# Low-rank FFN: stacked fp32r parts of the first product, and the inner layer's product with 64-row halves

## The reference, cut to what matters

```
def _L1_ffn_ref(x, U1, V1, b1, U2, V2, b2):
    D_MODEL, D_FF, RANK = (256, 1024, 64)
    B, S = (4, 1024)
    P = jnp.einsum('bsd,dr->bsr', x, U1)
    H = jax.nn.gelu(jnp.einsum('bsr,rf->bsf', P, V1) + b1)
    Q = jnp.einsum('bsf,fr->bsr', H, U2)
    return jnp.einsum('bsr,rd->bsd', Q, V2) + b2
...
x = x + _L1_ffn_ref(_layernorm(x, axis=-1), L1_ffn_U1, ..., L1_ffn_b2)   # block six (s5F), block eight (s7F)
```

## Time and profile before

| | before |
|---|---|
| median of 3 runs | 3765.04 us |
| span of the profiled execution | 3759.3 us |
| TensorE matmul busy | 3174.3 us (84%) |
| VectorE busy | 2380.3 us (63%) |
| ScalarE busy | 2097.1 us (56%) |
| GpSimd busy | 844.5 us (22%) |
| mean granted TensorE clock | 0.93 |

### The profile page before, as it was taken

One profiled execution on the slowest core, in us unless ns is written; L12 is line 12 of the kernel. 1 busy time (PEld: TensorE's weight loads), 2 busy tenths in 40 slices (PEclk: granted clock), 3 DMA queues, 4 the chain that ended last, 5 costly groups with the idle time before them and its releaser, 6 DMA issues. The chain is left out here.

```text
span 3759.3 us, 71272 instructions
## 1 busy us (share of the span) xinstructions
PE 3174.3 (84%) x21288; PEld 2152.6 (57%) x21288; DVE 2380.3 (63%) x5292; ACT 2097.1 (56%) x3482; POOL 844.5 (22%) x1652
## 2 busy tenths in 40 slices
PE   6699999999999639996883599959688888797879
PEld 3366666666666339996441499944355555533433
DVE  4488888888886664444567644435477677435853
ACT  3589989898987224442221344422266666354544
POOL 2211111111110114443001244524422222120112
PEclk9899999999999769998896799979899899898889
DMA  3300000000000314433003244331211111100001
GB/s 116 101 22 25 25 25 22 25 25 25 22 24 16 113 52 90 90 79 74 9 0 113 66 92 91 73 81 62 83 51 51 47 52 52 24 0 12 0 18 39
DMA packets 148659, 186.76 MB, mean 50 GB/s; under 512 B 20304, under 2 KB 114768, under 8 KB 148560
## 3 DMA queue, kind: packets, MB, share of 16 engines
q1 hardware_dynamic: 123984, 151.94, 12.6%
q0 software_dynamic: 24576, 33.57, 5.5%
HBM read 122.54 MB, written 62.91 MB: 49 GB/s over the span
## 5 line engine op out<-in xcount | busy, mean ns | idle before, releaser
L1717 DVE CUSTOM_DVE_ANT_0 s0Ah_SD<-s0Ah_ps_s,s0Ah_table 128x1024 f32<-128x1024 f32 x512 | 623.3, 1218 | 40.1 <-PE s0Ah_ps_s L1808 25.2
L1763 ACT ACTIVATE s0Ah_PM<-s0Ah_SD,s0Ah_nb 128x1024 f32<-128x1024 f32 x512 | 594.6, 1161 | 24.6 <-POOL s0Ah_nb L1706 24.6
L1818 PEld LDWEIGHTS s0Ah_ps_t<-top_ident,s0Ah_PM 128*128 128x128 f32 x4096 | 480.8, 141 | 103.0 <-ACT s0Ah_PM L1763 3.4
L1818 PE MATMUL s0Ah_ps_t<-top_ident,s0Ah_PM 128*128 128x128 f32 x4096 | 533.8, 273 | 0.4
L1769 ACT COPY s0Ah_PT<-s0Ah_ps_t 128x512 f32<-128x512 f32 x512 | 302.9, 592 | 104.3 <-PE s0Ah_ps_t L1818 99.8
L2021 ACT ACTIVATE s4Ch_PM<-s4Ch_SD,s4Ch_nb 128x260 f32<-128x260 f32 (+2 forms) x512 | 254.3, 497 | 145.7 <-POOL s4Ch_nb L1964 132.3
L1808 PE MATMUL s0Ah_ps_s<-s0Ah_ks,s0Ah_qs 96*128 96x512 bf16 x1024 | 308.5, 383 | 28.2 <-DMA s0Ah_ks<-s0A_parts 27.5
L1725 DVE COPY s0Ah_PT<-s0Ah_ps_t 128x512 f32<-128x512 f32 x384 | 264.9, 690 | 94.7 <-PE s0Ah_ps_t L1818 91.9
L1706 POOL TENSOR_TENSOR s0Ah_nb<-s0Ah_mx,s0Ah_minus 128x1 f32<-128x1 f32 x512 | 98.2, 192 | 930.5 <-DVE s0Ah_mx L1717 930.5
L1831 PE MATMUL s0Ah_ps_v<-s0Ah_PT,s0Ah_Vs 128*32 128x512 f32 x2048 | 273.9, 607 | 0.0
L1975 DVE CUSTOM_DVE_ANT_0 s4Ch_SD<-s4Ch_ps_s,s4Ch_table 128x260 f32<-128x260 f32 (+2 forms) x512 | 205.1, 408 | 79.8 <-PE s4Ch_ps_s L2066 65.2
(11 more groups left out here) (389 smaller groups left out, 7432.8 us busy)
## 6 DMA issues: line engine op xcount, KB each, us to landing
s1M_raw_w<-in_L_ffn_w SPq DMA_DIRECT2D x16, 1024.0 KB
s3M_raw_w<-in_L_ffn_w SPq DMA_DIRECT2D x16, 1024.0 KB
s0A_parts<-s0Ap_sp SPq DMA_DIRECT2D x48, 256.0 KB, 2.4
s4C_parts<-s4Cp_sp SPq DMA_DIRECT2D x48, 256.0 KB, 2.4
s0Ah_qs<-s0A_parts SPq DMA_DIRECT2D x64, 96.0 KB
s0Ah_ks<-s0A_parts SPq DMA_DIRECT2D x64, 96.0 KB
s4Ch_qs<-s4C_parts SPq DMA_DIRECT2D x64, 96.0 KB
s4Ch_ks<-s4C_parts SPq DMA_DIRECT2D x64, 96.0 KB
```

What stands on the lines that cost most here:

```text
L1717: nc.vector.tensor_tensor_reduce(SD[u % NBUF][:, :], ps_s[u % 2][:, :, :].rearrange("p a n -> p (a n)"), table[:, (TB - 1 - t) * P:(TB - 1 ...
L1763: nc.scalar.activation(PM[u % NBUF][:, :], SD[u % NBUF][:, :], ACT.Exp, bias=nb[:, u:u + 1]).then_inc(e_ok, 1)
L1818: x = nc.tensor.transpose(ps_t[:, bank, k * P:(k + 1) * P], PM[u % NBUF][:, at:at + P], ident[:, :])
```

## The change

Only `low_rank_ffn` changes, with the same lines for both stages.

- U1 is loaded twice, into both halves of 128 columns. `first` is now two full products that add up in `ps_p`, so that every partition half holds the whole P.
- ScalarE rounds P to fp32r: `PA` on all partitions, and the lower half of `PB`. VectorE writes the rest, P minus its rounded part, to the upper half of `PB`. V1 is split once into `v1_top` (ScalarE) and `v1_rest` (VectorE).
- `hidden` does two blocks in a call: each block is `v1_top` times `PB` over all 128 rows (top times top plus top times rest), then `v1_rest` times `PA` over 64 rows, the first block on partitions 0 to 63, the second on 64 to 127. It signals once for two blocks. There are four PSUM buffers for it instead of two.
- `ps_t` and `ps_o` shrink to one bank each. The transposes of a group are done in two calls of four.
- The loops are written out, and the order on every engine is new: the outputs of group g-1 are now in turn g, the transposes of g+2 lie within the turn, and VectorE adds group g-1 before LayerNorm of g+2.

```diff
-    u1 = ph.sb("u1", [P, DC, R])
+    u1 = ph.sb("u1", [P, DC, P])
+    v1_top, v1_rest = ph.sb("v1_top", [P, FF], F32R), ph.sb("v1_rest", [P, FF], F32R)
-    PT, QT = ph.sb("PT", [P, GT]), ph.sb("QT", [P, GT])
+    PA = [ph.sb(f"PA{i}", [P, GT], F32R) for i in range(2)]
+    PB = [ph.sb(f"PB{i}", [P, GT], F32R) for i in range(2)]
-    ps_t = ph.ps("ps_t", [P, DC, GT])
+    ps_t = ph.ps("ps_t", [P, GT])
-    ps_h = ph.ps("ps_h", [P, 2, GT])
+    ps_h = ph.ps("ps_h", [P, NH, GT])
-    ps_o = ph.ps("ps_o", [P, 2, GT])
+    ps_o = ph.ps("ps_o", [P, GT])
...
         @block.vector
         def _(dve):
+            def rest_of(g):
+                dve.wait_ge(top_ok, START + 2 * g + 2)
+                nc.vector.tensor_tensor(PB[g % 2][R:P, :], ps_p[R:P, :], PA[g % 2][R:P, :].bitcast(F32),
+                                        ALU.subtract).then_inc(rest_ok, 1)
+
+            def added(g):
                 dve.wait_ge(b_add, START + g + 1)
                 for k in range(G // 2):
                     dve.wait_ge(o_mm, START + g * (G // 2) + k + 1)
...
+            ln.vector(dve, 0)
+            dve.wait_ge(vt_ok, START + 1)
+            nc.vector.tensor_tensor(v1_rest[:, :], v1[:, :], v1_top[:, :].bitcast(F32), ALU.subtract).then_inc(vr_ok, 1)
+            ln.vector(dve, 1)
+            rest_of(0)
+            for g in range(NG):
+                if g:
+                    added(g - 1)
+                if g < NG - 2:
+                    ln.vector(dve, g + 2)
+                if g < NG - 1:
+                    rest_of(g + 1)
+            added(NG - 1)
...
         @block.scalar
+            def tops(g):
+                act.wait_ge(p_mm, START + g + 1)
+                nc.scalar.copy(PA[g % 2][:, :], ps_p[:, :]).then_inc(top_ok, 1)
+                nc.scalar.copy(PB[g % 2][0:R, :], ps_p[0:R, :]).then_inc(top_ok, 1)
...
+            for g in range(NG):
+                for m in range(4):
+                    hidden(g, m)
+                if g < NG - 2:
+                    turned(g + 2, 0)
+                for m in range(4, 6):
+                    hidden(g, m)
+                if g < NG - 1:
+                    tops(g + 1)
+                for m in range(6, 8):
+                    hidden(g, m)
+                if g < NG - 2:
+                    turned(g + 2, 1)
                 act.wait_ge(q_mm, START + g + 1)
                 act.wait_ge(o_mm, START + g * (G // 2))
                 nc.scalar.copy(QT[:, :], ps_q[:, :]).then_inc(q_sb, 1)
...
         @block.tensor
+            def turned(g, c):
+                if c == 0:
+                    pe.wait_ge(ln.hrow, START + (g + 1) * G)
+                pe.wait_ge(ln.hTok, START + g * DC + c)
+                for j in range(G):
+                    x = nc.tensor.transpose(ps_t[:, j * P:(j + 1) * P], ln.h[0][:, j, c * P:(c + 1) * P], ident[:, :])
+                x.then_inc(ln.trans, 1)
...
             def hidden(g, m):
-                pe.wait_ge(h_sb, START + g * M + m - 1)
-                nc.tensor.matmul(ps_h[:, m % 2, :], v1[:, m * P:(m + 1) * P], PT[:, :],
-                                 start=True, stop=True).then_inc(h_mm, 1)
+                if m == 0:
+                    pe.wait_ge(rest_ok, START + g + 1)
+                pe.wait_ge(h_sb, START + g * M + m + 2 - NH)
+                for j in range(2):
+                    nc.tensor.matmul(ps_h[:, (m + j) % NH, :], v1_top[:, (m + j) * P:(m + j + 1) * P], PB[g % 2][:, :],
+                                     start=True, stop=False)
+                for j in range(2):
+                    half = slice(j * R, (j + 1) * R)
+                    x = nc.tensor.matmul(ps_h[:, (m + j) % NH, :], v1_rest[half, (m + j) * P:(m + j + 1) * P],
+                                         PA[g % 2][half, :], start=False, stop=True)
+                x.then_inc(h_mm, 1)
...
+            for g in range(NG):
+                hidden(g, 0)
+                if g:
+                    outs(g - 1, 0)
+                hidden(g, 2)
+                if g:
+                    outs(g - 1, 1)
+                down(g, 0)
+                if g < NG - 2:
+                    turned(g + 2, 0)
+                hidden(g, 4)
+                down(g, 2)
+                if g < NG - 1:
+                    first(g + 1)
+                hidden(g, 6)
+                if g < NG - 2:
+                    turned(g + 2, 1)
+                down(g, 4)
+                down(g, 6)
+            outs(NG - 1, 0)
+            outs(NG - 1, 1)
```

More of the change, by code:

```diff
@@ L167, in low_rank_ffn @@
     M = FF // P
+    NH = 4
     hT = ph.sb("hT", [P, 2, DC, GT])
-    u1 = ph.sb("u1", [P, DC, R])
+    u1 = ph.sb("u1", [P, DC, P])
     v1 = ph.sb("v1", [P, FF])
+    v1_top, v1_rest = ph.sb("v1_top", [P, FF], F32R), ph.sb("v1_rest", [P, FF], F32R)
     bias1 = ph.sb("bias1", [P, M])
@@ L244, in _ @@
         def _(act):
-            act.wait_ge(weights, loaded)
[L247 to L256, removed]
+            def turned(g, c):
+                act.wait_ge(ln.trans, START + g * DC + c + 1)
+                nc.scalar.copy(hT[:, g % 2, c, :], ps_t[:, :]).then_inc(ln.hTok, 1)
@@ new lines, in _ @@
+            act.wait_ge(weights, loaded)
+            nc.scalar.copy(v1_top[:, :], v1[:, :]).then_inc(vt_ok, 1)
+            for g in range(2):
+                for c in range(DC):
+                    turned(g, c)
+                if g == 0:
+                    tops(0)
+            for g in range(NG):
[11 more added lines that the diff above has]
+                    turned(g + 2, 1)
@@ L291, in down @@
                                          start=(m == 0), stop=(m == M - 2), tile_position=(0, j * R))
                 if m == M - 2:
-                    i.then_inc(q_mm, 1)
-            def turn(g, h, following, more):
-                pe.wait_ge(p_sb, START + g + 1)
-                pe.wait_ge(q_sb, START + g)
-                for m in range(M):
-                    hidden(g, m)
-                    if m >= 3 and m % 2:
-                        down(g, m - 3)
-                if more:
-                    ln.tensor(pe, g + 2)
-                down(g, M - 2)
-                if following:
-                    first(g + 1, 1 - h)
-                pe.wait_ge(q_sb, START + g + 1)
-                pe.wait_ge(o_add, START + g * (G // 2))
-                for k in range(G // 2):
-                    for j in (2 * k, 2 * k + 1):
-                        i = nc.tensor.matmul(ps_o[:, k, (j % 2) * D:(j % 2 + 1) * D], QT[:, j * P:(j + 1) * P],
-                                             v2[:, :], start=True, stop=True)
-                    i.then_inc(o_mm, 1)
@@ L314, in _, with outs @@
-            ln.tensor(pe, 0)
-            ln.tensor(pe, 1)
-            first(0, 0)
-            skewed_turns(pe, turn)
+                    x.then_inc(q_mm, 1)
+            def outs(g, k):
+                n = g * (G // 2) + k
+                pe.wait_ge(q_sb, START + g + 1)
+                pe.wait_ge(o_add, START + n)
+                for j in range(2):
+                    at = (2 * k + j) * P
+                    x = nc.tensor.matmul(ps_o[:, j * D:(j + 1) * D], QT[:, at:at + P], v2[:, :], start=True, stop=True)
+                x.then_inc(o_mm, 1)
```

66 lines of the change are left out of this document (34 added, 32 removed).

## The result

| | before | after |
|---|---|---|
| median (lowest to highest of 4 runs) | 3765.28 us (3763.25 to 3765.86) | 3838.33 us (3822.0 to 3838.65) |
| ratio after / before | | 1.0195, 95% interval 1.0177 to 1.0213 |
| span of the profiled execution | 3759.3 us | 3820.0 us |
| mean granted TensorE clock | 0.93 | 0.918 |
| s5F, first statistics to end of last add | 3269.79 to 3410.68: 140.9 us | 3263.85 to 3439.77: 175.9 us |

The change makes the kernel slower, by 73 us in the medians. The profiled execution of after is the run of 3822.0 us; the other three took 3838.1 to 3838.7 at a mean granted clock of 0.913 to 0.914, against 0.918 in the profiled one. Where in the kernel those 16 us lie was not found, for only one of the four has a trace. The profile is therefore compared with its own span: 60.7 us over before.

The account below looks back on a forecast made before the run. TensorE's matmul stream was taken as the bound, 15.36 us a turn; new waits and lost clock gave +29.1 us per stage, +58.2 for two, span 3817.5, plus 5.7 to the median: 3823 us, range 3785 to 3850.

Parts of the forecast that it names:

- The wait: TensorE before the transposes of g+2: idle for VectorE's add and LayerNorm rows, 6.7 us in each of turns 1 to 5.
- The way from the outputs to the add: From the end of outputs' second half on TensorE to the start of VectorE's add: 0.4 us.
- The clock: TensorE after each wait: part of the work at 1.2 GHz, losing 1.6 to 2.9 us, 2.1 taken.
- The loop at full clock: From the transposes of g+2 to the next such start: 11.5 us of TensorE work plus 7.74, 19.3 us.
- the rival of a clock that stays up, at 3798 us: TensorE keeps full clock over the wait: loss of 2.1 gone six times per stage, +33 us for two; chance 0.2.
- Work of a turn: TensorE's matmul work in one FFN turn: 11.2 us plus seven further shape changes, 12.4 us, 3.0 less than before.
- the changes of shape: TensorE switching between array shapes in a turn: about 0.17 us for each change.
- Row halves: A pair of 64-row halves in the hidden product: one slot, 0.23 us, with two, 0.46, as the other end.
- The rival at 3838 us: Hidden product: the 64-row halves don't run side by side, +15 us; chance 0.15.
- Start and end: Each FFN stage: transposes of group 2 start 15.65 us after the first; turn 6 takes 12.3 us, turn 7 15.3.
- The sum: Both FFN stages with start, five loops and end: +29.1 us per stage, +58.2 for two.
- The faster rival, at 3721 us: The LayerNorm chain doesn't hold the transposes and matmul work rules: turn 12.4 us, -44 us for two stages; chance 0.05.

Follow-up runs that it names:

- e4_late: The changed kernel with the transposes of the next group moved late in TensorE's and ScalarE's turn, VectorE's order kept; 3737.14 us, ratio 0.9944.
- e8_bias_late: The changed kernel with GpSimd's bias add for g held until VectorE has written the normalized rows of g+2; 3796.05 us, ratio 1.0110.
- e1_filler: The changed kernel with 26 unused fp32r matmuls issued on TensorE before it waits for LayerNorm rows in turns 1 to 5; 3799.71 us, ratio 1.0122.
- e5_late_moments: Against e4_late, VectorE's statistics of g+2 moved ahead of the adds of g-1, the row writes left behind them; 3729.46 us, ratio 0.9941.
- e7_full_rows: Against e5_late_moments, each pair of 64-row halves replaced by two products over all 128 rows, lower half of weights zero; 3728.56 us, ratio 0.9924.
- e6_same_rows: Against e5_late_moments, both 64-row halves of every pair taken from the same rows 0 to 63; 3744.74 us, ratio 0.9964.

## Why the forecast held, and where its steps were off

The time lies in the range, 3838 against 3823 us forecast, and the mechanism named is the one the runs show: VectorE's chain became a wait of TensorE, and the clock fell behind it. How close the sum came is partly luck. For the profiled execution 3817.5 us were forecast and 3820.0 measured, but the two stages grew by 69.0 us instead of 58.2, and the 8.3 us by which the unchanged stages were shorter hid most of that; and the median lies 16 us above this execution for a reason that was not found.

- The wait. Forecast 6.7 us idle in five turns; measured 6.34 in four and 8.37 in the fifth (the same in s7F), with 0.86 before the first transposes of the loop. The chain was taken at 7.29 + 0.05 us from the earlier trace rows and was 7.31. The way from the outputs to the add was put at 0.4 and was 0.1: down 0 starts at 3304.40, the add at 3304.51. e4_late proves the step from the other side: with the same chain, other place, 0.44 us.
- Missed: the contended rows in the last LayerNorm turn. The 3.31 us of the earlier trace rows had the bias add in it, and the prediction named that. But in the last such turn GpSimd has no further power to wait for, two bias adds follow each other (4.68 us), and the rows beside them take 5.42. That is 2.03 us per stage; e8_bias_late removed it. Timeline of after:

```profile
3395.60 4.68 POOL L221 TENSOR_TENSOR top_X<-top_X,s5F_bias 128x1024 f32<-128x1024 f32 x2
3395.66 5.42 DVE L113 TENSOR_SCALAR s5F_ln_h<-top_X,s5F_ln_mv,s5F_ln_rstd 128x256 f32<-128x256 f32 x4 [1.41 <-POOL s5F_ln_rstd L123]
...
3401.14 1.11 PE L300 MATMUL s5F_ps_t<-top_ident,s5F_ln_h 128*128 128x128 f32 x4 [8.37 <-DVE s5F_ln_h L113]
```

- The clock. Taken from the six resumptions of s6D as 1.6 to 2.9, 2.1 on average; measured 1.3 to 2.9, mean 2.2, over the eight loops that follow a wait of 6.34 us. The waits of s6D were 2.6 to 4.9 us, so that they gave the right loss for a longer wait was not known beforehand. The loss in the first loop was counted in the forecast and came, but it followed the slow start of the stage and not a wait of the new order. The loop at full clock was put at 19.3 and is 19.47 in e1_filler. So the rival of a clock that stays up, at 3798 us, fell, but it was priced somewhat too low: e1_filler, which is that case for most of the turns, has 1.0122 times 3765 = 3811 us, with the doubled bias adds, the half clock in the first loop and the longer start and end in it.
- Work of a turn. Forecast 12.4 us, measured 13.12 in e5_late_moments. The columns are right; the changes of shape are not. The f32 slots (four down, four first, two pairs of outputs, eight transposes) are 7.74 us, the fp32r columns 4 x 0.70, so 2.6 us are left for changes where 11 x 0.17 = 1.9 stood. The mis-sized term is the 64-row form, by e7_full_rows. In the changed kernel the error was nearly hidden, since what it adds to the loop (0.5) stood against 0.3 that the way to the add fell short.
- Row halves. One slot for two was taken, and e6_same_rows shows it: serial halves cost 0.85 us a turn. The rival at 3838 us gave the measured time by a mechanism that e6_same_rows rules out; its number coming out is no support for it.
- Start and end. The first transposes came 10.59 us after the first statistics (9.91 forecast, 9.41 before), from there to the transposes of group 2 it took 16.32 (15.65), and from the last transposes to the end 38.63 (37.45). Together 2.5 us per stage too few.
- The sum. 29.1 forecast per stage, 35.0 measured in s5F. The 5.9 between are: 3.4 in the five loops (110.4 against 107.0; 2.0 of it the doubled bias adds), 1.35 in the start, 1.2 in the end. In s7F 34.0 were measured, 4.9 more than forecast: 10.8 for the two stages. The 8.3 us by which the rest is shorter have no cause in the change; no run explains them.
- The faster rival, at 3721 us, was the case that the LayerNorm chain does not hold the transposes. It did not come in the changed kernel, and e4_late and e5_late_moments are that case: 0.994 times 3765 is 3743 us. It is less than the rival gave in part because a turn saves 2.24 and not 2.96 us: by the rival's own sum that makes -32 us instead of -44. The traces of e5_late_moments have -28.9 in the two stages, the timed ratio -22 (between -14 and -31); what lies between was not settled.

## What to carry to other kernels

A chain of small steps over several engines costs nothing while its consumer stands late enough in the bottleneck engine's program; when outputs and LayerNorm are reordered, measure the chain once (7.3 us here) and count the products between its first and last step. A wait on TensorE is paid twice where the clock falls behind it: 6.3 us of waiting cost 1.3 to 2.9 more, 0.44 us cost nothing. Before packing half-height products side by side, compare with full-height ones padded with zeros: here the padding was as fast, for the 64-row form was as dear as the columns saved.

## What the runs showed of the hardware

- Matmuls whose result nobody uses can save time: 26 of them in a wait of 6.3 us took the turn from between 21.0 and 22.4 us down to 19.47 us, since the granted clock stayed at 1.00 instead of 0.52 over the next 6.8 us.
- TensorE was fully busy for 6.78 us at a mean granted clock of 0.52 after idle stretches of 6.3 us, and lost nothing measurable after one of 0.44 us in a turn of 13.65, where the clock read 1.00.
- A row write of 0.40 us on VectorE, SBUF to SBUF, stood for 2.44 us beside a GpSimd addition of 2.34 us; with the addition held back none of 28 took over 0.414.
- A pair of 64-row fp32r products between full-row ones costs 0.26 us beyond its columns (a turn of 13.12 us, against 13.03 with full-row products that have 0.95 us more of columns).
- Two fp32r products of 64 rows in different halves of the array take 0.50 us together, in the same half 0.73.
